# The attention layer of a graph network: two passes over the edges and a stage between them, rewritten as one pass

## The reference, cut to what matters

```python
xl = (x @ Wl + bl).reshape(n, HEADS, C)
xr = (x @ Wr + br).reshape(n, HEADS, C)
ee = (eattr @ We).reshape(-1, HEADS, C)
msg = xl[src_a] + xr[dst_a] + ee
score = einsum('ehc,hc->eh', leaky_relu(msg, 0.2), att)
smax = segment_max(score, dst_a, num_segments=n)
ex = exp(score - smax[dst_a])
denom = segment_sum(ex, dst_a, num_segments=n)
alpha = ex / (denom[dst_a] + 1e-16)
out = segment_sum(alpha[:, :, None] * xl[src_a], dst_a, num_segments=n)
```

## Time and profile before

| what | us |
|---|---|
| median of three runs | 6556.79 |
| lowest and highest run | 6548.45, 6574.01 |
| span of the profiled execution (first to last instruction) | 5097.6 |
| median less this span | 1459.2 |
| stage 1, `layer3_nodes`, 2984 to 3027 | 43 |
| stage 2, `score_pass`, 3027 to 4219 | 1192 |
| stage 3, `segment_weights`, 4219 to 4300 | 81 |
| stage 4, `weighted_pass`, 4300 to 4944 | 644 |
| stage 5, `node_tail`, 4944 to 5097.6 | 153.6 |

### The profile page before, as it was taken

How to read it: one execution, slowest core, us unless ns; L and a number is a source line. 1 busy time by engine, 2 the same in 40 slices (tenths; PEclk the granted TensorE clock), 3 DMA queues, 4 the chain that set the end, 5 groups by cost and what they waited for, 6 DMA issues and landing times. The chain is left out here.

```text
span 5097.6 us, 87677 instructions
## 1 busy us (share of the span) xinstructions
PE 3793.2 (74%) x18006; PEld 2595.3 (51%) x18007; DVE 3316.9 (65%) x9829; ACT 1463.6 (29%) x3497; POOL 2922.7 (57%) x2917
## 2 busy tenths in 40 slices
PE   0477777777678888599779989888999973555563
PEld 0466666666444444355446655555555542444441
DVE  5788888888798888333242244544545446788878
ACT  1355555555344444000000022222222221000012
POOL 1577777777377777777500017777777770333334
PEclk9755555555688888799889985555555555999986
DMA  6677777777533332498566636666666673655530
GB/s 121 193 248 247 248 249 246 247 249 247 161 100 97 98 98 79 101 196 197 125 202 202 202 109 178 176 175 175 176 178 177 175 160 79 157 142 144 142 100 25
DMA packets 1057652, 843.56 MB, mean 165 GB/s; under 512 B 546808, under 2 KB 952812, under 8 KB 1044022
## 3 DMA queue, kind: packets, MB, share of 16 engines
q1 hardware_dynamic: 785634, 597.46, 39.2%
q0 software_dynamic: 98096, 176.73, 13.5%
q10 hardware_dynamic: 173844, 68.53, 5.5%
HBM read 601.34 MB, written 167.28 MB: 151 GB/s over the span
## 5 line engine op out<-in xcount | busy, mean ns | idle before, releaser
L2317 POOL DMA_INDIRECT ring<-xl_rows,idx x896 | 893.9, 998 | 786.5 <-DVE idx L2396 513.7
L434 POOL DMA_INDIRECT ringa<-x_sign_pos,idxa x880 | 870.8, 990 | 303.3 <-issue 296.3
L986 POOL DMA_INDIRECT edge_counts<-edge_cnt,places x832 | 824.2, 991 | 358.1 <-issue 269.9
L2389 PE MATMUL zps<-We,eaT 64*128 64x128 f32 x1792 | 711.0, 498 | 0.0
L2663 PE MATMUL ops<-val,hot 128*128 128x200 f32 x1792 | 370.2, 351 | 273.1 <-DVE out L2682 241.8
L2387 PE MATMUL zps<-xr,hotT 128*128 x2688 | 454.4, 302 | 144.6 <-ACT hotT L2369 83.2
L2419 DVE TENSOR_TENSOR z<-zps,ring 128x512 f32<-128x512 f32 x224 | 154.9, 692 | 601.9 <-PE zps L2389 478.6
L2389 PEld LDWEIGHTS zps<-We,eaT 64*128 64x128 f32 x1792 | 447.6, 309 | 163.5 <-issue 145.4
L2630 POOL TENSOR_TENSOR val<-rows,val 128x512 f32<-128x512 f32 x224 | 234.9, 1049 | 507.3 <-ACT val L2649 379.3
L519 PE MATMUL sela<-hota,endsa 128*128 128x128 f32 x1760 | 408.5, 405 | 133.6 <-ACT endsa L460 120.3
L2663 PEld LDWEIGHTS ops<-val,hot 128*128 128x128 f32 x1792 | 302.2, 194 | 341.0 <-DVE out L2682 307.0
(11 more groups left out here) (367 smaller groups left out, 5978.6 us busy)
## 6 DMA issues: line engine op xcount, KB each, us to landing
edge_counts<-zeroa SPq DMA_DIRECT2D x55, 1568.0 KB
matd<-edge_counts SPq DMA_DIRECT2D x12, 6272.0 KB
keyb<-edge_keys SPq DMA_DIRECT2D x50, 1216.0 KB
dstb<-dst_in_tile SPq DMA_DIRECT2D x112, 512.0 KB
xl_of_steps<-ring SPq DMA_DIRECT2D x224, 256.0 KB
rows<-xl_of_steps SPq DMA_DIRECT2D x224, 256.0 KB
reseta<-resets SPq DMA_DIRECT2D x110, 512.0 KB
dstba<-dst_in_tile_bf ACTq DMA_DIRECT2D x112, 256.0 KB
```

Source lines behind the costliest of these rows:

```text
L434: p.indirect_dma_start(out=ring[:, k, :], out_offset=None, in_=table, in_offset=bass.IndirectOffsetOnAxis(ap=idx[:, k:k + 1], axis=0)).the ...
L986: p.indirect_dma_start(out=g.M.rearrange("d s -> (d s)").unsqueeze(1), out_offset=bass.IndirectOffsetOnAxis(ap=g.place[:, c:c + 1], axis=0 ...
L2317: p.indirect_dma_start(out=ring[:, c, k, :], out_offset=None, in_=g.xl_rows[0:N, :], in_offset=bass.IndirectOffsetOnAxis(ap=idx[:, q * GS ...
L2389: ins = t.matmul(zk, eaT[:, c, k, :], g.We[:, :], start=False, stop=True)
```

## The change

`score_pass`, `segment_weights` and `weighted_pass` are replaced by one function, `fused_pass`. What it does differently:

- The rows of xl are gathered once and stay in SBUF, in a ring of 16 groups, until they are summed. They are neither written to DRAM nor read back. Their multiplication by the weights moves from GpSimd to VectorE.
- The message is built transposed (features on partitions, edges along the columns) in one PSUM bank `zT`: four fp32 transposes of the gathered rows, two fp32 products with We (the host lays the edge attributes out in halves for it), and twelve bf16 products with the pieces of xr as the stationary operand.
- ScalarE copies 0.2 times `zT` to SBUF (`low`). VectorE takes the larger of `low` and `zT` (`lk`).
- The sum over a head is a matmul with a column of att, so the scores of a turn collect in one PSUM bank `S3`, 128 rows (head, step) by 128 edges.
- The segment maxima are found per turn with scans over 128 elements, a chain of twelve small operations carries them over the steps and from turn to turn, and the sums of the open node are rescaled when the maximum moves on.
- The one-hot `hot` of the sums is built on ScalarE (four Abs, one Relu) and no longer on VectorE.
- The sums of a group follow 12 groups behind its message (LAG), in the same body.
- x is written to DRAM in `layer3_nodes` and read back in `node_tail`; its place is scratch in between. `node_tail` loads xl and xr itself. Setting up We and att takes a memset and seven small DMAs, where it was two.

The core of the diff (`older` is true except in the first groups, `new` is false in the steps behind the last group):

```diff
+HC = U3 * HEADS
+SLOT = FX + DE
+RINGS = 2 * NG3
+LAG = NG3 + 4
...
-def score_pass(nc, g, a):
-def segment_weights(nc, g):
-def weighted_pass(nc, g, a):
+def fused_pass(nc, g, a):
...
+            @block.scalar
...
+                def onehot(it, q):
+
+                    W, half, of = it * BODY + q - LAG, (q - LAG) // NG3 % 2, (q - LAG) % NG3 * GS
+                    if of == 0:
+                        s.wait_ge(s_minus, it * 2 + (q - LAG) // NG3 + 1)
+                    wait(s, s_hot, W)
+                    for k in range(GS):
+                        s.activation(apart[:, k * P:(k + 1) * P], g.iota_n[:, :], ACT.Abs, bias=minus[:, half, of + k:of + k + 1]
+                                     ).then_inc(s_far, 1)
+                    wait(s, s_o, W - 1)
+                    wait(s, s_far, (W + 1) * GS)
+                    s.activation(hot[:, q % 2, :, :], apart.rearrange("p (k n) -> p k n", k=GS), ACT.Relu, scale=-1.0, bias=1.0
+                                 ).then_inc(s_hot, 1)
+
+                def step(it, q, new=True):
...
+                        s.activation(apartT, dstb[:, h, off:off + GS * P], ACT.Abs, bias=nodes[:, :]).then_inc(s_apart, 1)
+                        wait(s, s_z, G - 1)
+                        wait(s, s_apart, G + 1)
+                        s.activation(hotT[:, c, :], apartT, ACT.Relu, scale=-1.0, bias=1.0).then_inc(s_hotT, 1)
+                    if turn and q % NG3 == 3:
+                        weights(it, q)
+                    if older(it, q, 1) and (new or q == 0):
+                        wait(s, s_z, G)
+                        wait(s, s_lk, G - 2)
+                        s.activation(low[:, 1 - c, :], zT[1 - c][:, :], ACT.Copy, scale=0.2).then_inc(s_low, 1)
+                    if older(it, q, LAG) and (new or q < LAG):
+                        onehot(it, q)
...
+            @block.tensor
...
+                def messages(it, q):
+                    G, b = it * BODY + q, q % 2
+                    t.load(regs, g.T[0:1, bass.ds(G * GS, GS)])
+                    T = [t.snap(r, min_val=0, max_val=NT - 1) for r in regs]
+                    wait(t, s_lk, G - 1)
+                    t.wait_ge(s_g[q], 64 * (it + 1))
+                    for k in range(GS):
+                        t.matmul(zT[b][:, k * P:(k + 1) * P], ring[:, q * GS + k, 0:F], g.ident[:, :], is_transpose=True,
+                                 start=k == 0, stop=False, skip_group_check=True)
+                    t.wait_ge(s_ea[q], 64 * (it + 1))
+                    for i in range(2):
+                        t.matmul(zT[b][:, :].rearrange("f (k i e) -> f k i e", i=2, e=DE)[:, :, i, :], g.Wpad[:, i, :],
+                                 ring[:, slots(q), FX:SLOT], start=False, stop=False, skip_group_check=True)
+                    wait(t, s_hotT, G + 1)
+                    for k in range(GS):
+                        for i in range(3):
+                            ins = t.matmul(zT[b][:, k * P:(k + 1) * P], g.xr3[:, bass.ds(T[k] * (3 * F) + i * F, F)],
+                                           hotT[:, b, k * P:(k + 1) * P], start=False, stop=i == 2, skip_group_check=True)
+                    ins.then_inc(s_z, 1)
+
+                def scores(it, q):
+
+                    G, b, o = it * BODY + q - 1, (q - 1) % 2, (q - 1) % NG3
+                    t.wait_ge(s_lk, G + 1)
+                    if o == 0:
+                        wait(t, s_S, it * 2 + (q - 1) // NG3)
+                    for k in range(GS):
+                        c = o * GS + k
+                        at = U3 - 1 - c
+                        ins = t.matmul(Sps[:, 0:P], g.attcol[:, at:at + HC], lk[:, b, k * P:(k + 1) * P],
+                                       start=c == 0, stop=c == U3 - 1)
+                    ins.then_inc(s_sc, 1)
...
+                    wait(t, s_hot, W + 1)
+                    wait(t, s_val, W + 1)
+                    wait(t, s_out, (W - 1) * GS)
+                    for k in range(GS):
+                        ins = t.matmul(ops[b][k // 2][:, (k % 2) * FX:(k % 2 + 1) * FX], hot[:, b, k, :],
+                                       ring[:, (q - LAG) % BODY * GS + k, 0:FX], start=True, stop=True)
+                    ins.then_inc(s_o, 1)
...
+                def step(it, q, new=True):
+                    if older(it, q, LAG) and (new or q < LAG):
+                        weighted(it, q)
+                    turn = older(it, q, NG3) and (new or q < NG3)
+                    if turn and q % NG3 == 1:
+                        four(it, q)
+                    if turn and q % NG3 == 2:
+                        bounds(it, q)
+                    if older(it, q, 1) and (new or q == 0):
+                        scores(it, q)
+                    if turn and q % NG3 == 3:
+                        turned(it, q)
+                    if new:
+                        messages(it, q)
...
+            @block.vector
...
+                def leaky(it, q):
+
+                    G, b = it * BODY + q - 1, (q - 1) % 2
+                    v.wait_ge(s_low, G + 1)
+                    v.wait_ge(s_z, G + 1)
+                    wait(v, s_sc, G - 1)
+                    v.tensor_tensor(lk[:, b, :], low[:, b, :], zT[b][:, :], ALU.max).then_inc(s_lk, 1)
...
+                def product(it, q):
...
+                    of = ring[:, r, 0:F].rearrange("p k (h c) -> p k h c", c=C)
+                    v.tensor_tensor(of, of, ring[:, r, F:F + HEADS].unsqueeze(3).broadcast_to([P, GS, HEADS, C]), ALU.mult
+                                    ).then_inc(s_val, 1)
...
+                def step(it, q, new=True):
+                    if older(it, q, LAG) and (new or q < LAG):
+                        product(it, q)
+                    if older(it, q, 1) and (new or q == 0):
+                        leaky(it, q)
+                    if older(it, q, LAG + 1):
+                        add(it, q)
...
+                if older(it, q, BODY):
+                    s.wait_ge(s_o, G - BODY + 1)
...
+                s.dma_start(g.x3.rearrange("(t p) f -> p t f", p=P), g.x[:, :, :]).then_inc(s_spill, 16)
...
-                p.wait_ge(g.s_early, 16 * 6)
+                    p.wait_ge(s_lr[lo // LT], 32)
```

More of the change, by code:

```diff
@@ new lines, in step, with body @@
+                    if older(it, q, LAG) and (new or q < LAG):
+                        onehot(it, q)
+                    if turn:
+                        if q % NG3 == 0:
+                            score_copy(it, q)
+                        if q % NG3 == 2:
+                            factor(it, q)
+                        if q % NG3 == 3:
+                            weights_out(it, q)
+                def body(it):
+                    for q in range(BODY):
+                        step(it, q)
@@ new lines, in four, with bounds @@
+                def four(it, q):
+                    j, half = it * 2 + q // NG3 - 1, 1 - q // NG3
+                    t.wait_ge(s_v, j * LINKS + AT_FOUR)
+                    for i, of in enumerate((run[:, P - 1:P], early[:, P - 1:P], top[:, 0:1], reset[:, half, 0:1])):
+                        ins = t.matmul(misc[0:1, i * HC:(i + 1) * HC], of, g.ident[:, :], start=True, stop=True)
+                    ins.then_inc(s_four, 1)
+                def bounds(it, q):
+                    j = it * 2 + q // NG3 - 1
+                    t.wait_ge(s_v, j * LINKS + AT_CARRY)
+                    for i in range(2):
+                        ins = t.matmul(misc[:, 2 * P + i:2 * P + i + 1], carry[0:1, i, :, :].rearrange("o h c -> o (h c)"),
+                                       g.ones[0:1, 0:1], start=True, stop=True)
+                    ins.then_inc(s_bound, 1)
@@ new lines, in _, with next_indices @@
+                v.memset(g.out[:, :], 0.0).then_inc(s_ini, 1)
+                v.wait_ge(s_ini, 2)
+                regs = [v.alloc_register(f"a3{j}") for j in range(GS)]
+                tile = v.alloc_register("r3")
+                L, B = slice(0, U3 - 1), slice(1, U3)
+                def next_indices(it, q):
+                    j, half = it * 2 + q // NG3, q // NG3
+                    v.wait_ge(s_z, j * NG3)
+                    v.tensor_copy(idx[:, 1 - half, :], g.src_f[:, bass.ds((j + 1) * U3, U3)]).then_inc(s_idx, 1)
@@ new lines, in add @@
+                def add(it, q):
+                    W, b = it * BODY + q - LAG - 1, (q - 1) % 2
+                    v.load(regs, g.T[0:1, bass.ds(W * GS, GS)])
+                    T = [v.snap(r, min_val=0, max_val=NT - 1) for r in regs]
+                    wait(v, s_o, W + 1)
+                    for k in range(GS):
+                        wait(v, s_out, W * GS + k)
+                        to = g.out[:, bass.ds(T[k] * FX, FX)]
+                        v.tensor_tensor(to, to, ops[b][k // 2][:, (k % 2) * FX:(k % 2 + 1) * FX], ALU.add).then_inc(s_out, 1)
@@ L2698, in node_tail @@
+                turns(v, body, LAST)
+                for q in range(LAG + 1):
+                    step(LAST, q, False)
+                v.wait_ge(s_out, TURNS3 * NG3 * GS)
```

618 lines of the change are left out of this document (259 added, 359 removed).

## The result

| | kernel before | changed kernel |
|---|---|---|
| median, us | 6552.84 (4 runs) | 6645.98 (4 runs) |
| lowest to highest | 6548.45 to 6574.01 | 6624.01 to 6660.61 |
| ratio, 95% interval | | 1.0134, 1.0105 to 1.0163 |
| span of the profiled execution | 5097.6 | 6622.3 |
| granted clock over the span | | 0.738 |

The change made the kernel slower by 1.3%, 93 us. The forecast was +329.

A forecast was written before the change was run, and what follows sets the result against it. TensorE's work plus its wait for `hot`, under a mixed clock, was taken to bound the fused loop: 2226 for `fused_pass` + 20 around it - 1917 removed = +329 us, 6886 us; 8-in-10 range 6420 to 7150.

The forecast's parts named there:

- The minus term: The three replaced stages, whose time in the first profile was taken off whole: 1917 us.
- Score pass at GpSimd's pace: In the old score pass, gathers 1.25 us apart, four a group, set the pace: 1120 of 1192 us.
- The closed loop: In each group TensorE's sums wait for `hot`, made behind `low` and the previous messages: 2.9 us, between 2.5 and 3.3.
- TensorE's work: TensorE's busy time per group in the fused loop: 5.3 us at the high clock, 5.1 before the turn's extras.
- The sum for the low clock: TensorE's work per group in the fused loop at 1.2 GHz: about 9.2 us.
- the rival of the low clock: TensorE's clock stays low throughout the fused loop: 12.1 us a group, +866 us, 7423 us; chance 0.10.
- The clock: Every second pause in the fused loop costs TensorE 3 us at low clock: 1.5 us a group, mean near 0.7.
- The cycle: One group of the fused loop takes 9.7 us, bounds 8.2 and 12.1; 224 groups make 2173 us.
- Around it: Outside the fused loop, writing x 12, the tail's own loads 5, setting up We and att 3: 20 us.
- The chain: VectorE's chain of maxima, 9 us a turn, is covered by TensorE's messages and pause; uncovered it would cost 250 us.
- The clock did not hold: Rival: TensorE's clock stays high in the fused loop, 8.2 us a group or less, 6393 to 6550 us; chance 0.18.
- The loop was closed: Rival without a closed loop: TensorE runs through at 5.3 us a group, -657 us, 5900 us; chance 0.07.

The follow-up runs named there:

- (1): The kernel before, unchanged, run again for a second profile: 6512.91 us, its three stages 2230 us.
- (4): The changed kernel, unedited, run again for a profile on the same chip as (1): 6557.59 us.
- (16): The changed kernel, unedited, a third time on another chip: 6524.78 us, ratio 1.0036 to the kernel before.
- (2): The changed kernel with the making of `hot` moved to the head of ScalarE's step: 6035.99 us, ratio 0.9277 to the kernel before.
- (7): The changed kernel with the four Abs of `hot` done twice, once into spare memory: 6957.91 us, ratio 1.0711 to the kernel before.
- 14: The changed kernel with 13 small unread fp32 matmuls ahead of TensorE's wait for `hot`: 6291.95 us, ratio 0.9678 to the kernel before.
- (3): The changed kernel with one copy in VectorE's chain of maxima done seven times a turn: 6613.31 us, ratio 1.0167 to the kernel before.
- (6): (2) with TensorE's scores two groups behind the messages and ahead of the sums: 5929.22 us, ratio 0.9132 to the kernel before.
- (9): (6) with VectorE's product and ScalarE's `hot` made one step ahead of the sums: 5855.22 us, ratio 0.9006 to the kernel before.
- 5: The changed kernel with `hot` built by one comparison on VectorE again: 6081.34 us, ratio 0.9367 to the kernel before.
- 15: (9) with 12 more already satisfied semaphore waits a step on ScalarE: 5864.17 us, ratio 0.9013 to the kernel before.
- 10: The changed kernel with 60 small unread bf16 matmuls ahead of TensorE's wait for `hot`: 6527.25 us, ratio 1.0048 to the kernel before.
- (12): (6) with 12 small unread bf16 matmuls ahead of TensorE's wait for `hot` and the product: 5976.62 us, ratio 0.9202 to the kernel before.

## Why the prediction was right or wrong

**The minus term was wrong; this step failed.** The prediction took off "all three stages, 1917 us", and left "the 1459.2 us between that span and the median of the three runs as they are". The 1917 us are those of an execution that the timed ones don't resemble; in these the stages take 2230 us (1). With that term and everything else as predicted the sum is 2226 + 20 - 2230 = +16 us, and the comparisons (4) and (16) measured +47 and +19. The term was 313 us too small, more than the whole miss of 236 us in the first comparison. The other 77 us, the other way, are the new stage, 2321 us and not 2226, less the 20 us around it that are not seen. So it is in part luck that the time went the way that was forecast: with the right term the same working says +16 us, no change. The hint stood in the table: a span 22% below the time of every run.

**Score pass at GpSimd's pace: true only of the first profile.** In the earlier trace rows gathers followed each other at 1.25 us, and the stage took 5.3 us a group. In (1) a group takes 6.7 us, and TensorE waits for edge attributes.

**The closed loop: right.** Shown by taking it away (2, -522 us) and by the dose (7). Its length was too small: 3.4 to 3.6 us in the mean over 212 groups of each of the three executions, 2.9 predicted, 2.5 to 3.3 as bounds. In the group shown above, products' end 5029.21, `low` 5030.09, Abs 5030.59 to 5031.85, Relu to 5032.51, sums 5032.65: from `low` to the end of the Relu it is 2.42 us, 2.45 predicted; the step to the sums is 0.14 and not 0.24. What was too small is the first part, 0.88 us to the start of `low` (0.9 to 1.1 in the mean) where 0.24 was taken.

**TensorE's work: too large.** At the high clock 5032.65 to 5037.12, 4.5 us, 5.1 predicted without the turn's extra matmuls. Most of it is the twelve products, 0.83 us and not 1.3. They cost half of their low-clock price, the lower of the two ends. The sum for the low clock was added up wrongly: 9.7 less 0.6 and with 0.3 is 9.4 and not 9.2 (9.5 measured), and the rival of the low clock would be 12.3 us a group.

**The clock: right in kind.** 1.5 us a group and a mean near 0.7 were predicted; the groups at either level give 1.8 us in the first execution, at a mean of 0.80. The stage of 14, at 0.94, is 216 us shorter than that of 16 at 0.82, 1.0 us a group. The Trainium skill, "TensorE: Matmul & The Clock Gate", section "A second HAM failure mode: psum-queue depth-cycling", has it that TensorE's clock can go back and forth when it idles briefly between groups of matmuls; by that rule both levels could appear, and the trace agrees, 0.53 and 1.00 in neighbouring groups. What the same page of the Trainium skill says of transposes and the clock ("Part 4: PE-mode transpose") no run here can show: the transposes always stand between other matmuls.

**The cycle: right, 10.06 us (9.8 and 9.9 in the repeats) for 9.7,** which is in part luck: the pause was taken 0.7 too short, the work at the high clock 0.7 too long, and the clock's share 0.3 too short. The stage came out within 4%.

**Around it: too large.** 20 us predicted, nothing seen.

**The chain: covered, as predicted, by 2.9 us.** In no group did the sums wait for it; a chain 3.8 us a turn longer outgrew the cover (3).

**The rivals.** The clock did not hold (0.80), and it did not stay low. The loop was closed in this kernel; kernels without it were built in (2), (6) and (9), and even in (9) TensorE does not run through, at 7.0 us a group and not 5.3.

**What stays open.** What the stalls are that the profile puts down to "issue" and "remote", why the first profiled execution had so much less of them, and why the loads of the edge attributes are late in (1). Some expectations speak of the supply of instructions; no run shows it. The stalls do not follow the number of instructions of ScalarE (5, 15), and on TensorE they come with many small matmuls in a row (10 against 14). In the changed kernel they come at the same places of every turn: `low` starts 1.8 to 2.1 us behind the products in two groups of eight, and 0.3 to 1.0 us in the others. The stalls hold ScalarE's `low` back and are the likely reason why (9) is not at 5.3 us a group; that was only argued.

## What to carry to other kernels

Set the profiled span against the times before summing anything: if it is far below them, take a second profile, since stage lengths can be far off (here 1192 against 1509 us, and 442 against 790). A lag of twelve groups does nothing when the producer stands, on its own engine, behind a wait for the group just finished; find for each wait what its producer is queued behind, and move the producer ahead. Where a pause can't be removed, cheap work in few instructions that keeps TensorE busy can pay (14); where the pauses were irregular it cost time (12).

## What the runs showed of the hardware

- One execution of a program was more than a fifth shorter (span 5097.6 us) than all others of it (6465 to 6574 us), with the same instructions. In it 330 matmuls of 385 columns ran without a gap; in a later one some 150 of them stood alone, most 2.8 us apart.
- 60 small bf16 matmuls in a row are not fed evenly: 35 of them in 1.84 us, then single ones 0.7 us apart; in 196 of 224 groups they were interrupted. 26 fp32 records of like total length ran through in every group, in 3.09 us in the one shown.
- 2.8 us a group of work that nobody reads made the kernel 3.6% faster than without it (0.9678 against 1.0036), since the clock of the stage went from 0.82 to 0.94.
- 12 satisfied semaphore waits a step on ScalarE, 2700 in all, cost 9 us (5864 against 5855, on one chip, in two groups of runs with 6506 and 6501 for the kernel before).
